# A deformable convolution pipelined with a ternary Winograd convolution: a reordered head, levelled offset taps, x1 read two chunks ahead, w1 and w2 prepared elsewhere, and no one-element memsets

## The chip, the cores and the metric

The kernel runs on one core of one Trainium2 chip. Its time is the device time of one execution in microseconds (us). The engines are TensorE (PE in the profile; PEld are its weight loads), VectorE (DVE), ScalarE (ACT), GpSimd (POOL) and SyncE (SP), which issues most DMAs; GpSimd issues the gathers.

## The reference, cut to what matters

x is (4, 256, 64, 64) in float32: 4 batches, 256 channels, 64 rows of 64 pixels. There are two layers, each on a group-normalised input and with a residual.

```python
def deform(x, w_off, b_off, w_conv):            # layer 0
    om = conv3x3(x, w_off) + b_off              # 27 channels: 18 offsets, 9 masks
    mask = sigmoid(om[:, 18:])
    # per pixel and tap k (9): a position (y, x), four neighbours, four weights
    sampled = bilinear(x, ys, xs) * mask        # zero outside the image
    return einsum("bckhw,ock->bohw", sampled, w_conv)

def ternary(w):                                 # to -1, 0, 1
    w = w - w.mean(); third = (w.max() - w.min()) / 3
    return where(w < w.min() + third, -1, where(w > w.max() - third, 1, 0))

def block(x, w1, g1, b1, w2, g2, b2):           # layer 1
    out1 = relu(batchnorm(conv3x3(x, ternary(w1)), g1, b1))
    out2 = batchnorm(conv3x3(out1, ternary(w2)), g2, b2)
    return relu(out1 + out2)

x = x + deform(group_norm(x), w_off, b_off, w_conv)
x = x + block(group_norm(x), w1, g1, b1, w2, g2, b2)
```

## The kernel before

Work is cut into chunks of 8 rows (512 pixels), 8 to a batch, 32 in all; the 256 channels are two halves of 128 partitions. The order of the work is written out by hand: each engine has a queue of its own, and semaphores tie them together. In the first part `schedule` walks over stages s = 0 to 4, and in each over 8 chunks. One chunk step does four things at once: `z`, the statistics of x for batch s+2; `o`, the offset convolution and the table of batch s+1; `d`, the sampling and the deformable convolution of batch s; `f`, the first convolution of layer 1 (Winograd, ternary weights w1) of batch s-1. Stage 4 has `f` alone. Each step is cut into nine slots k = 0 to 8, one to a tap. The loop over chunks is peeled: some chunks stand written out, the rest in a hardware loop.

*Sampling* (`d`). The normalised x stands in HBM as a table `pixel_pairs` with one row for each pixel position, which holds the four neighbours (1024 floats). For each tap GpSimd issues four indirect DMAs (L447), 128 rows of 4 KB each, into a ring `G` of 12 slots. VectorE combines them (L961): four multiply-adds 512 wide, then four 256 wide, and behind each four a one-element memset into a tile `pause` (L963). ScalarE multiplies by the last weight (L551). TensorE transposes (L1169) into `psT`, ScalarE copies that to `ST` (L607), and TensorE multiplies with `wconv` into `psD` (L1077), one tap behind the transposes. Slots of `G` come free with the transposes, three taps behind. At k = 0 `finish_deform` waits for the last tap of the chunk before, adds x (L818, into `x1c`) and takes statistics. Sampled rows go to HBM as x1.

*Offsets* (`o`). TensorE runs the nine offset taps into `psA` (L1046, `O_TAPS`: three at k=0, two at each of k=1..3). ScalarE evacuates (`om_evac`, k=4), TensorE turns (`turn_om`, k=5, L1085), ScalarE applies the sigmoid (`om_turned`, k=6), and VectorE makes row numbers and weights in two halves (`o_indices`, k=7 and k=8; L845 to L867). The convolution reads x in two parts, high and low, made by `split_hi` (ScalarE) and `split_lo` (VectorE, L771). TensorE also turns the pixels (L1196) for the table, which SyncE writes with four DMAs a chunk (`write_table`, L363).

*Head and batch 0.* Batch 0 has nobody ahead of it. In the head its statistics are taken, x is normalised in place in `G` (L496), turned (L1119) and written to the table, and its offsets are made for two chunks; for the other six, `j` work runs inside the chunk steps of stage 0, two chunks ahead: `jt_conv` at k=0..3 (`J_TAPS`, L1095), evacuation at k=4, turn at k=5, sigmoid at k=6, `jt_indices` at k=7, 8, and `jt_split` for the chunk three ahead at k=7 (L881, L888). w1 is loaded whole in the head; VectorE reduces it to sum, maximum and minimum (`weight_sums`, L668 to L670), compares (L699, L700) and transforms it there. GpSimd starts sampling when the table, its border (16 DMAs) and the indices of chunk 0 are ready. SyncE's queue in the head: x of batch 0, small constants, w1, two chunks of x of batch 1, the border, then the table rows with the other loads between them.

*Stage 4.* Eight chunks of `f`: x1 is loaded (L345) and normalised (L537), VectorE forms four planes (`planes`, L785), ScalarE copies their high part (L614), VectorE forms the low part (`planes_lo`, L794), TensorE convolves into `psF` and `psD` (L1065), and ScalarE and VectorE combine them to h1 rows (L622, L806 to L811), which SyncE stores. The load of the next chunk is issued one step ahead. In this stage w2 is loaded whole into `G`, reduced (L668 to L670, 4608 elements a partition), compared and transformed by VectorE. The second part of the kernel (L1286 on) is the second convolution and the end.

Of the kernel before, what the change touches and what calls it, by code (L numbers as in the profile page):

```python
# [14 lines left out]
def build(nc, x, w_off, b_off, w_conv, w1, w2, bn_params, ident, group_avg, sel_hl, base, out):  # L15
# [6 lines left out]
    ds = bass.ds  # L22

    NB, C, H, W = 4, 256, 64, 64
    CT = C // 128
    TAPS = 9
# [50 lines left out]
    with outer, names:  # L77
# [42 lines left out]
        with one:  # L120
# [19 lines left out]
            xres, xz = xx[:, 0], [xx[:, 3], xx[:, 1]]  # L140
# [17 lines left out]
            wst = sb(one, "wst", [128, 3, 3])  # L158
            wmm = sb(one, "wmm", [2, 4])
            wall = sb(one, "wall", [128, 8])  # L160
            pause = sb(one, "pause", [128, 2 * TAPS])
# [12 lines left out]
            ps_w_row = [psD[0:2, 0, 0:128], psT[0:2, 0, 0:128]]  # L174
            ps_w = [psD[:, 1, 0:3], psT[:, 1, 0:3]]
# [6 lines left out]
            W1_SLOT = CT * H * W // (4 * C)  # L182
            raw1 = [(0, 0, 9, g_flat[:, CT * H * W:CT * H * W + 9 * C]), (1, 0, 7, g_flat[:, CT * H * W + 9 * C:CT * H * W + 16 * C]),
                    (1, 7, 9, x1c[:, 0, :])]
            above1 = po[:, 1].rearrange("p q t h w -> p (q t h w)")[:, 0:HW]
# [12 lines left out]
            raw_off = ST[:, 0, :, :].rearrange("p t x -> p (t x)")[:, 0:CT * TAPS * 27].rearrange(  # L198
                "p (t k j) -> p t k j", t=CT, k=TAPS)
            zero_sb = xf[:, 0, :, :, :].rearrange("p t h w -> p (t h w)")[:, 0:2 * C]  # L200
# [6 lines left out]
            s_init = sem("init_steps")  # L207
            s_tern, s_wtr, s_wrd = sem("ternary_done"), sem("w_sums_step"), sem("w_sums_turned")
# [10 lines left out]
            h_stat, s_w1 = sem("h_stats_done"), sem("w1_loaded")  # L219
# [28 lines left out]
            def schedule(eng, emit):  # L248
# [3 lines left out]
                for s in range(0, NB + 1):  # L252
                    def at(r, rh, p, first, last):
# [5 lines left out]
                        just = (ahead(r, rh, p, 2), ahead(r, rh, p, 3)) if s == 0 else (None, None)  # L259
# [5 lines left out]
                        emit(s, *now, *then, *just, before)  # L265
# [43 lines left out]
            def _(sp):  # L309
                for r in range(NR):  # L310
                    sp.dma_start(x_all[:, :, r * PX:(r + 1) * PX], rows_of(x, 0, r * RC, RC)).then_inc(h_load[r], 16)
                for dst, src in ((idn[:], ident), (gavg[:], group_avg), (selhl[:], sel_hl),
                                 (base_s[:].rearrange("p r i -> p (r i)"), base.rearrange("p r i -> p (r i)")),
# [70 lines left out]
                def emit(s, z, o, d, f, o2, f2, j, j2, fp):  # L384
# [14 lines left out]
                    if f2:  # L399
                        load_f(f2)  # L400
# [1116 lines left out]
```

## Time and profile before

| | us |
|---|---|
| median of 3 runs | 2930.91 (2930.48 to 2938.26) |
| profiled execution, its own time | 2936.16 |
| span of its instructions | 2934.3 |
| head, up to the first step of VectorE in stage 0 | 117.5 |
| stage 0 | 574.0 |
| stage 1 | 531.7 |
| stage 2 | 523.2 |
| stage 3, sampling | 506.0 |
| stage 4 behind it | 167.0 |
| second part | 514.9 |
| TensorE, VectorE, ScalarE, GpSimd busy | 2442, 2234, 1275, 1368 |

An engine's busy time is the time in which it executes; TensorE's matmuls overlap, so a busy TensorE is not one at its peak. The granted clock (PEclk) is TensorE's clock as a share of 2.4 GHz. The DMA share is the mean busy share of 16 DMA engines. In a timeline a row gives the start, the time from the first start to the last end, engine, line, operation, destination and source, and the number of instructions; brackets give the idle time ahead of it and what ended it. "SPq" is SyncE issuing DMAs.

### The profile page before, as it was taken

The numbers are of one execution on the slowest core, as the hardware profiler recorded it, in microseconds if no ns is written. First come the engines' busy times: TensorE is split into PE (matmuls) and PEld (weight loads), VectorE is DVE, ScalarE is ACT, GpSimd is POOL, SyncE is SP. The second block draws the span as 40 slices with busy tenths as digits, with TensorE's granted clock in tenths as the row PEclk, the third lists the DMA queues.
The fourth block names the chain that finished last, engine by engine and source line by source line (L and its number), as shares of the span: only waits on it lengthen the run. The fifth ranks groups of instructions, "written<-read, shape, count | busy, mean of one in ns | idle before, by whom it ended". The sixth has DMA issues, their size and how long they took to land. (4 is left out here: it accounts for less than half of the span.)

```text
span 2934.3 us, 38779 instructions
## 1 busy us (share of the span) xinstructions
PE 2442.2 (83%) x12442; PEld 1692.3 (58%) x12442; DVE 2234.0 (76%) x4734; ACT 1275.2 (43%) x2181; POOL 1367.5 (47%) x1262
## 2 busy tenths in 40 slices
PE   4288888888999999999999998889887677999930
PEld 3144444444566566556566665555555677999930
DVE  6667777777888888888888887888786664666566
ACT  3244444445644445555555444444443123233245
POOL 1345554555655555556556555666652003333300
PEclk9699999999999999999999998999998888999975
DMA  7788888899999999999999999999995112111179
GB/s 248 270 292 301 317 304 303 311 348 353 332 360 354 360 351 351 342 329 363 337 361 363 343 330 325 345 347 343 342 343 218 50 61 70 53 60 52 44 278 408
DMA packets 277755, 826.29 MB, mean 282 GB/s; under 512 B 25692, under 2 KB 59484, under 8 KB 276964
## 3 DMA queue, kind: packets, MB, share of 16 engines
q0 software_dynamic: 165888, 604.05, 55.0%
q1 hardware_dynamic: 111716, 220.47, 21.7%
q8 instruction: 64, 1.05, 0.1%
q14 instruction: 87, 0.71, 0.1%
HBM read 738.95 MB, written 85.48 MB: 281 GB/s over the span
## 5 line engine op out<-in xcount | busy, mean ns | idle before, releaser
L447 POOL DMA_INDIRECT G<-pixel_pairs,quad_c x1152 | 1204.9, 1046 | 896.7 <-PE psT L1169 582.8
L961 DVE SCALAR_TENSOR_TENSOR G<-G,wts_c 128x256 f32<-128x256 f32 (+1 forms) x2304 | 1258.4, 612 | 217.5 <-DMA G<-pixel_pairs,quad_c 212.2
L1077 PE MATMUL psD<-ST,wconv 128*128 128x512 f32 x2304 | 1079.1, 613 | 0.0
L551 ACT ACTIVATE G<-G,wts_c 128x256 f32<-128x256 f32 x1152 | 490.5, 497 | 496.6 <-DVE G L961 496.5
L1077 PEld LDWEIGHTS psD<-ST,wconv 128*128 128x128 f32 x2304 | 434.6, 199 | 444.9 <-issue 444.9
L1169 PE MATMUL psT<-idn,G 128*128 128x128 f32 x2304 | 323.5, 286 | 218.8 <-ACT G L551 216.6
L607 ACT ACTIVATE ST<-psT 128x1024 f32<-128x1024 f32 x288 | 294.1, 1021 | 419.4 <-PE psT L1169 419.2
L1169 PEld LDWEIGHTS psT<-idn,G 128*128 128x128 f32 x2304 | 269.8, 146 | 314.7 <-ACT G L551 185.2
L1065 PE MATMUL psF<-pl,qw 128*128 128x256 f32 x1872 | 267.6, 298 | 35.7 <-DVE h1c L809 24.9
L1065 PEld LDWEIGHTS psF<-pl,qw 128*128 128x128 f32 x1872 | 244.2, 195 | 53.3 <-DVE h1c L809 21.2
L1046 PE MATMUL psA<-po,woff 128*64 128x512 f32 x864 | 253.2, 437 | 0.0
L1474 PE MATMUL psG<-po,qw 128*128 128x256 f32 x1440 | 226.8, 286 | 24.7 <-POOL po L1325 24.7
L1474 PEld LDWEIGHTS psG<-po,qw 128*128 128x128 f32 x1440 | 197.8, 191 | 24.9 <-issue 24.9
L1046 PEld LDWEIGHTS psA<-po,woff 128*64 128x64 f32 x864 | 117.0, 136 | 108.0 <-issue 39.6
L1348 ACT ACTIVATE po<-area 128x1024 fp32r<-128x1024 f32 x48 | 49.2, 1056 | 250.8 <-PE psG L1474 242.2
L1474 PE MATMUL psG<-pg,qw 128*128 128x256 f32 x864 | 141.8, 285 | 0.0
L1325 POOL TENSOR_TENSOR po<-area,po 128x1024 fp32r<-128x1024 f32 x32 | 69.9, 2206 | 123.0 <-ACT po L1348 123.0
L818 DVE TENSOR_TENSOR x1c<-psD,xx 128x1024 f32<-128x1024 f32 x32 | 39.2, 1224 | 114.2 <-PE psD L1077 114.2
L1474 PEld LDWEIGHTS psG<-pg,qw 128*128 128x128 f32 x864 | 124.4, 189 | 0.0
L1402 DVE TENSOR_TENSOR area<-area 128x512 f32<-128x512 f32 x128 | 79.9, 686 | 51.2 <-POOL pg L1325 25.5
L561 ACT ACTIVATE yT<-psX 128x256 f32<-128x256 f32 x96 | 36.2, 377 | 167.3 <-PE psX L1196 166.8
L785 DVE TENSOR_TENSOR xx<-xf 128x512 f32<-128x512 f32 x128 | 80.0, 685 | 30.1 <-ACT xf L537 29.6
(214 smaller groups left out, 2241.0 us busy)
## 6 DMA issues: line engine op xcount, KB each, us to landing
xx<-in_x SPq DMA_DIRECT2D x56, 512.0 KB, 4.3
pixel_pairs<-yT SPq DMA_DIRECT2D x104, 256.0 KB, 7.2
G<-pixel_pairs,quad_c POOLq DMA_INDIRECT x1152, 6.6
x<-x1c SPq DMA_DIRECT2D x32, 512.0 KB
h<-h1c SPq DMA_DIRECT2D x32, 512.0 KB, 9.1
out<-h SPq DMA_DIRECT2D x16, 1024.0 KB, 17.3
xf<-x SPq DMA_DIRECT2D x24, 640.0 KB, 8.5
area<-h SPq DMA_DIRECT2D x24, 640.0 KB, 4.1
```

The lines of the kernel that those rows point to most:

```text
L447: pool.indirect_dma_start(out=G[:, i % RING, :], out_offset=None, in_=tbl[d.b].rearrange("y x q c -> (y x) (q c)"), in_offset=bass.Indirec ...
L551: act.activation(g, g, ACT.Copy, scale=wts_c[:, d.p, i:i + 1]).then_inc(d_scaled, 1)
L607: act.activation(ST[:, k % 3], psT[:], ACT.Copy).then_inc(d_st, 1)
L785: i = dve.tensor_tensor(V[:, :, j], xf[:, f.p, :, a:a + 7:2, :], xf[:, f.p, :, b:b + 7:2, :], op)
L961: dve.scalar_tensor_tensor(g[:, 0:w], g[:, w:2 * w], wts_c[:, d.p, q * NG + i:q * NG + i + 1], g[:, 0:w], ALU.mult, ALU.add).then_inc(d_ma ...
L1046: ins = pe.matmul(acc[:, oc, :].rearrange("p (h w) -> p h w", h=RC), w[:, t, tap, oc * m:(oc + 1) * m], pad[:, c.p, part, t, dy:dy + RC, d ...
L1065: ins = pe.matmul(acc[:, bank, half * 256:half * 256 + 256].rearrange("p (h w) -> p h w", w=W), w[:, oc * 128:(oc + 1) * 128], p[:, part, ...
L1077: ins = pe.matmul(psD[:, oc, :], wconv[:, t, k, oc * 128:(oc + 1) * 128], ST[:, k % 3, t, :], start=(k == 0 and t == 0), stop=(k == TAPS - ...
L1169: ins = pe.transpose(psT[:, c, t * 128:(t + 1) * 128], G[:, (PT * k + t) % RING, c * 128:(c + 1) * 128], idn[:])
L1325: i = pool.tensor_tensor(pg(c.p, 1, t)[:, :, 1:W + 1], V[:, t].rearrange("p j i w -> p (j i) w"), pg(c.p, 0, t)[:, :, 1:W + 1].bitcast(F32 ...
L1402: i = dve.tensor_tensor(V[:, :, j], xg[:, c.p, :, a:a + 2 * RP - 1:2, :], xg[:, c.p, :, b:b + 2 * RP - 1:2, :], op)
L1474: i = pe.matmul(psG[:, c.p, oc, j, :].rearrange("p (h w) -> p h w", h=RP), w[:, oc * 128:(oc + 1) * 128], pg(c.p, part, t)[:, RP * j:RP * ...
```

## The change

In the sampling the memsets into `pause` are gone. In the head, VectorE takes statistics before any constant is needed, and the offset weights are split behind them. SyncE loads small constants first, then x; it loads four chunks of batch 1 at once into four buffers, then x for offset chunk 2, then writes the border of batch 0 alone; the borders of the other batches and `wconv` come behind the table. w1 is no longer in the head: it is loaded in six pieces (twice, once for the reductions and once for the comparison), and VectorE works on two pieces at a time in stage 0: reductions at k=3 of chunks 0, 3 and 4, comparisons at k=1 and k=6 of chunk 6 and k=6 of chunk 7, the transform at k=7 of chunk 7. Offset taps are spread anew, the offset work of batch 0 is shifted by half a step, and both halves of `o_indices` stand at k=8. w2 is reduced in six pieces in stage 3 (chunks 4 and 5, k=1, 3, 5); its comparison and transform run on GpSimd at the start of stage 4. In stage 4 x1 is loaded and normalised two chunks ahead. Stages 3 and 4 are peeled by five chunks instead of three.

VectorE's memset, and the walk and the taps:

```diff
-                                dve.memset(pause[:, 2 * k + q - 1:2 * k + q], 0.0)
...
-                    walk(eng, at, 5 if s == 0 else 3)
-            J_TAPS = {0: [0, 1], 1: [2, 3], 2: [4, 5], 3: [6, 7, 8]}
-            O_TAPS = {0: [0, 1, 2], 1: [3, 4], 2: [5, 6], 3: [7, 8]}
+                    walk(eng, at, 3 if 0 < s < NB - 1 else 5)
+            J_TAPS = {5: [0, 1], 6: [2, 3], 7: [4, 5], 8: [6, 7, 8]}
+            O_TAPS = {0: [0], 1: [1, 2], 2: [3, 4], 3: [5, 6], 4: [7, 8]}
```

SyncE, head:

```diff
+                for dst, src in ((idn[:], ident), (gavg[:], group_avg)):
+                    sp.dma_start(dst, src).then_inc(s_small, 16)
                 for r in range(NR):
                     sp.dma_start(x_all[:, :, r * PX:(r + 1) * PX], rows_of(x, 0, r * RC, RC)).then_inc(h_load[r], 16)
...
-                    for t, k0, k1, raw in raw1:
-                        sp.dma_start(raw, w1.rearrange("(t c) k o -> c t (k o)", c=128)[:, t, k0 * C:k1 * C]).then_inc(s_w1, 16)
-                    load_z(Chunk(1, 0, 0, 0, True, False))
-                    load_z(Chunk(1, 1, 0, 1, False, False))
-                    table_border()
+                    for r in range(4):
+                        load_hz(r)
+                    load_j(Chunk(0, 2, 1, 0, False, False))
+                    sp.wait_ge(s_zero, 6)
+                    table_border(0, s_edge)
                     for r in range(NR):
                         sp.wait_ge(h_yt, 2 * (r + 1))
                         write_table(0, r, yt_ring[r % 4], h_tw[r % 4])
...
+                        if r < 4:
+                            load_hz(r + 4)
+                        if r == 4:
+                            load_o(Chunk(1, 0, 0, 0, True, False))
+                    sp.dma_start(wconv[:].rearrange("p t k o -> p (t k o)"),
+                                 w_conv.rearrange("(t c) k o -> c t (k o)", c=128)).then_inc(s_wconv, 16)
+                    for b in range(1, NB):
+                        table_border(b, s_edge_rest)
+                    sp.wait_ge(z_stat, 2 * NR + CREDIT)
+                    load_w1(0)
```

SyncE, each step:

```diff
-                    if f2:
+                    if f2 and (s < NB or f.first):
                         load_f(f2)
+                    if s == NB and f2 and not f2.last:
+                        load_f(f2.after())
```

GpSimd:

```diff
+                def w2_ternary():
+                    pool.wait_ge(s_lim, 1)
+                    pool.wait_ge(s_wraw, 16)
+                    pool.tensor_scalar(above2, stage2, wall[:, 3:4], wall[:, 6:7], ALU.subtract, ALU.is_gt)
+                    pool.tensor_scalar(stage2, stage2, wall[:, 3:4], wall[:, 5:6], ALU.subtract, ALU.is_lt).then_inc(s_w2, 1)
+                    pool.wait_ge(s_w2, 1)
+                    pool.tensor_tensor(above2, above2, stage2, ALU.subtract).then_inc(s_w2, 1)
...
+                    pool.tensor_tensor(both, g[0], g[2], ALU.add).then_inc(s_w2, 1)
+                    pool.wait_ge(s_w2, 3)
+                    pool.tensor_tensor(minus, both, g[1], ALU.subtract)
+                    pool.tensor_tensor(g[1], both, g[1], ALU.add).then_inc(s_w2, 1)
+                    pool.wait_ge(s_w2, 4)
+                    pool.tensor_scalar(minus, minus, 0.5, None, ALU.mult)
+                    pool.tensor_scalar(g[1], g[1], 0.5, None, ALU.mult).then_inc(s_tern, 1)
```

ScalarE, each step:

```diff
+                        if jp and k == 1:
+                            jt_om_evac(jp)
+                        if j and k == 1:
+                            jt_normalise(j)
+                        if jp and k == 3:
+                            jt_om_turned(jp)
-                        if o and k == 4:
+                        if o and k == 5:
                             om_evac(o)
...
-                        if o and k == 6:
+                        if o and k == 7:
                             om_turned(o)
```

VectorE, each step:

```diff
+                        if s == NB - 1 and k in (1, 3, 5) and (d.is_row(4) or d.is_row(5)):
+                            part = k // 2 + (3 if d.is_row(5) else 0)
+                            dve.wait_ge(s_w2l, 48 if d.is_row(4) else 96)
+                            weight_sums(part, w2_part[k // 2]).then_inc(s_w2p, 1)
...
-                        if o and k in (7, 8):
-                            o_indices(o, k - 7)
-                        if j and k in (7, 8):
-                            jt_indices(j, k - 7)
-                        if j2 and k == 7:
-                            jt_split(j2, xf_rows(j2))
+                        if o and k == 8:
+                            o_indices(o, 0)
+                            o_indices(o, 1)
+                        if j and k == 2:
+                            jt_split(j, xf_rows(j))
+                        if jp and k in (4, 5):
+                            jt_indices(jp, k - 4)
+                        if s == 0 and k == 3:
+                            for r, p0, loaded in ((0, 0, 32), (3, 2, 64), (4, 4, 96)):
+                                if d.is_row(r):
+                                    dve.wait_ge(s_w1, loaded)
+                                    for part in (p0, p0 + 1):
+                                        weight_sums(part, w1_part[part % 2]).then_inc(s_w1p, 1)
...
+                        if s == 0:
+                            for r, kk, p0, loaded in ((6, 1, 0, 128), (6, 6, 2, 160), (7, 6, 4, 192)):
+                                if d.is_row(r) and k == kk:
+                                    dve.wait_ge(s_w1, loaded)
+                                    compare_w1(p0)
+                                    compare_w1(p0 + 1)
+                        if s == 0 and k == 7 and d.is_row(7):
+                            dve.wait_ge(s_w1p, 12)
+                            winograd_w1()
```

TensorE, each step:

```diff
-                            if k == 5 and j:
-                                jt_turn_om(j)
-                            if k == 5:
+                            if k == 2 and jp:
+                                jt_turn_om(jp)
+                            if k == 6:
                                 pe.wait_ge(o_yt, PT * (o.n + 1))
```

## Rows read from the trace of the kernel before

**Rows 1.** Busy time of each engine by stretch, granted clock, DMA share, GB/s

```profile
core 0: us, PE busy (x) PEld busy (x) DVE busy (x) ACT busy (x) POOL busy (x), PEclk, DMA share, GB/s
0.00:117.50 117.50, 35.94 (x161) 25.49 (x161) 77.05 (x147) 30.68 (x49) 15.72 (x16) 0.80 0.71 232
117.50:566.20 448.70, 372.62 (x1427) 209.38 (x1428) 327.93 (x812) 189.00 (x365) 229.35 (x227) 0.92 0.85 308
...
691.50:1223.20 531.70, 495.64 (x2301) 313.75 (x2300) 458.39 (x1056) 272.67 (x501) 305.31 (x299) 0.99 0.94 351
...
2252.40:2419.40 167.00, 111.98 (x800) 110.34 (x798) 110.79 (x153) 40.38 (x52) 0.05 (x1) 0.83 0.22 73
```

**Rows 2.** Timeline of the head

```profile
17.62 1.02 DVE L660 MEMSET woff<- 128x1152 f32 x1 [17.62 <-DMA boff<-in_b_off]
...
19.77 9.59 DVE L902 BATCH_NORM_STATS2 st<-G 128x6 f32<-128x512 f32 x16
...
32.58 4.34 ACT L496 ACTIVATE G<-G,bij,scj 128x512 f32<-128x512 f32 x6 [0.43 <-DVE bij L760]
...
102.24 4.29 SPq L363 DMA_DIRECT2D pixel_pairs<-yT  x4
...
110.31 0.21 POOL L440 COPY quad_c<-quad 128x36 int32<-128x36 int32 x1 [99.10 <-DMA pixel_pairs<-yT]
```

**Rows 3.** Timeline of TensorE in chunk 3 of batch 0

```profile
352.49 3.09 PE L1046 MATMUL psA<-po,woff 128*64 128x512 f32 x12
...
396.79 3.60 PE L1077 MATMUL psD<-ST,wconv 128*128 128x512 f32 x8
402.73 1.09 PE L1169 MATMUL psT<-idn,G 128*128 128x128 f32 x8 [2.35 <-ACT G L551]
403.66 5.29 PE L1077 MATMUL psD<-ST,wconv 128*128 128x512 f32 x8
416.15 1.97 PE L1169 MATMUL psT<-idn,G 128*128 128x128 f32 x8 [7.19 <-ACT G L551]
```

**Rows 4.** Timeline of VectorE in the same chunk, tap 8

```profile
411.22 3.14 DVE L961 SCALAR_TENSOR_TENSOR G<-G,wts_c 128x512 f32<-128x512 f32 x5
```

**Rows 5.** Timeline of TensorE in chunk 4 of batch 1

```profile
976.10 1.09 PE L1169 MATMUL psT<-idn,G 128*128 128x128 f32 x8 [0.77 <-ACT G L551]
...
1023.15 1.09 PE L1169 MATMUL psT<-idn,G 128*128 128x128 f32 x8 [1.75 <-ACT G L551]
...
1033.85 0.38 PE L1169 MATMUL psT<-idn,G 128*128 128x128 f32 x2
```

**Rows 6.** Timeline of stage 4

```profile
2283.09 4.93 DVE L668 TENSOR_REDUCE wst<-G 128x1 f32<-128x4608 f32 x1
...
2306.69 5.47 PE L1065 MATMUL psF<-pl,qw 128*128 128x256 f32 x24 [14.13 <-DVE h1c L809]
...
2398.97 5.40 PE L1065 MATMUL psF<-po,qw 128*128 128x256 f32 x24 [4.93 <-DVE h1c L809]
```

**Rows 7.** Timeline of VectorE, batch 1, five multiply-adds in a row

```profile
1027.30 3.15 DVE L961 SCALAR_TENSOR_TENSOR G<-G,wts_c 128x512 f32<-128x512 f32 x5
```

**Rows 8.** DMA issues: KB each, median us from issue to landing

```profile
G<-in_x SPq DMA_DIRECT2D x8, 512.0 KB, 7.7
```

**Rows 9.** Busy time by stretch, behind TensorE's wait in chunk 3

```profile
404.00:407.00 3.00, 3.00 (x5) 1.21 (x4) 2.67 (x10) 0.89 (x1) 2.30 (x3) 0.50 1.02 407
```

**Rows 10.** VectorE's groups in stage 4: busy, mean ns, idle

```profile
L699 DVE TENSOR_SCALAR G<-G,wall 128x4608 f32<-128x4608 f32 x1 | 2.7, 2678 | 0.0
```

**Rows 11.** GpSimd's groups

```profile
L1325 POOL TENSOR_TENSOR po<-area,po 128x1024 fp32r<-128x1024 f32 x32 | 69.9, 2206 | 123.0 <-ACT po L1348 123.0
...
L423 POOL MEMSET po<- 128x5280 f32 x1 | 4.5, 4512 | 0.0
```

**Rows 12.** Timeline of GpSimd, two gathers

```profile
120.55 0.94 POOL L447 DMA_INDIRECT G<-pixel_pairs,quad_c  x1 [0.30 <-issue]
121.80 1.40 POOL L447 DMA_INDIRECT G<-pixel_pairs,quad_c  x1 [0.31 <-issue]
```

More of the change, by code:

```diff
@@ L258, in at @@
                             then = (now[1] and now[1].after(), now[3] and now[3].after())
-                        just = (ahead(r, rh, p, 2), ahead(r, rh, p, 3)) if s == 0 else (None, None)
+                        just = [ahead(r, rh, p, n) if s == 0 else None for n in (2, 3, 1)]
                         f, before = now[3], None
@@ L404, in emit @@
                         load_j(j2)
+                    if s == 0 and d.is_row(6):
+                        sp.wait_ge(s_w1p, 8)
+                        load_w1(2)
                     if o:
@@ L442, in emit @@
                     for i in range(NG):
-                        if s == 0 and d.first and i == W1_SLOT:
-                            hold(pool, s_tern, 1)
                         if i % PT == RING % PT:
@@ L592, in emit @@
                     if f and not d:
+                        if f2 and not f2.last:
+                            normalise(f2.after(), xf, f_load, sc1, bi1, f_y, None)
                         h1_begin(s, f, 1)
@@ L672, in weight_sums_ready @@
                 def weight_sums_ready(parts):
-                    for part in range(1, parts):
-                        dve.tensor_tensor(wst[:, 0, 0:1], wst[:, 0, 0:1], wst[:, 0, part:part + 1], ALU.add)
-                        dve.tensor_tensor(wst[:, 1, 0:1], wst[:, 1, 0:1], wst[:, 1, part:part + 1], ALU.max)
-                        step(dve.tensor_tensor(wst[:, 2, 0:1], wst[:, 2, 0:1], wst[:, 2, part:part + 1], ALU.min))
-                    dve.tensor_scalar(wst[:, 2, 0:1], wst[:, 2, 0:1], -1.0, None, ALU.mult).then_inc(s_wtr, 1)
+                    for m, op in enumerate((ALU.add, ALU.max, ALU.min)):
+                        ins = dve.tensor_reduce(wst[:, m, 6:7], wst[:, m, 0:parts], AX.X, op)
+                    step(ins)
+                    dve.tensor_scalar(wst[:, 2, 6:7], wst[:, 2, 6:7], -1.0, None, ALU.mult).then_inc(s_wtr, 1)
                 def weight_extremes(m):
@@ L722, in compare_w1 @@
-                def compare_w1(part):
-                    t, k0, k1, raw = raw1[part]
-                    above = above1[:, 0:(k1 - k0) * C]
-                    compare(above, raw)
-                    step(dve.tensor_tensor(qw[:, t, k0:k1, :].rearrange("p k o -> p (k o)"), above.bitcast(F32), raw, ALU.subtract))
+                    dve.tensor_tensor(q, q.bitcast(F32), raw, ALU.subtract).then_inc(s_w1p, 1)
+                def winograd_w1():
+                    for t in range(CT):
+                        q = [qw[:, t, 3 * y:3 * y + 3, :].rearrange("p k o -> p (k o)") for y in range(3)]
+                        both, mid = w1_part
+                        dve.tensor_tensor(both, q[0].bitcast(F32), q[2].bitcast(F32), ALU.add)
+                        step(dve.tensor_scalar(mid, q[1].bitcast(F32), 0.5, None, ALU.mult))
+                        dve.scalar_tensor_tensor(wino[:, t].rearrange("p k o -> p (k o)"), both, 0.5, mid, ALU.mult, ALU.subtract)
+                        step(dve.scalar_tensor_tensor(q[1], both, 0.5, mid, ALU.mult, ALU.add))
+                    dve.sem_inc(s_tern, 1)
```

269 lines of the change are left out of this document (134 added, 135 removed).

## The prediction, made before the changed kernel was run

> **What bounds the kernel now.** I read the busy times by stretch first [rows 1], to see which engine has room in which stage. In the sampling of batch 1 TensorE is busy 495.6 of 531.7 us, and the DMA engines 0.94 of the time at 351 GB/s: two limits close together. In the first six chunks of batch 0 TensorE has 372.6 of 448.7 us and the DMA engines 0.85, so an order inside the chunk is at fault. In the stretch without sampling, 167 us, TensorE is busy 112 and the DMA engines 0.22. In the head TensorE works 35.9 of 117.5 us and VectorE 77.1.
>
> Then the timelines. In the head VectorE does nothing until 17.62 us, when the last small constant lands; its statistics begin at 19.77, ScalarE's first normalised rows at 32.58, and GpSimd's first copy of row numbers waits until 110.31 for the table, whose last row took SyncE 4.29 us for four DMAs [rows 2]. In a chunk of batch 0 TensorE waits 2.35 us for tap 7 and 7.19 for tap 8 [rows 3]: VectorE has splits and two halves of index chains between taps 7 and 8, and starts tap 8 at 411.22 only [rows 4]. In a chunk of batch 1 the waits are 0.77 us at tap 1 and 1.75 at tap 8 [rows 5]. In the last stretch chunk 2 begins at 2306.69, after a wait of 14.13 us, behind weight reductions that began at 2283.09, and chunk 7 at 2398.97: 18.5 us for each of five chunks [rows 6].
>
> **The change part by part.**
>
> *Memsets.* 576 go. One is queued between the fourth 512-wide and the first 256-wide multiply-add, and those five run in 3.15 us without a gap [rows 7]. The 0.06 us lie in the shadow of the neighbours; I take 0. Bounds: 0, and 576 x 0.06 = 34 us of gain were each on the path.
>
> *Head.* Statistics no longer wait for constants. The x loads land 7.7 us after issue in the median [rows 8], the last at about 15; with one pair of statistics behind it the chain is some 12.5 us earlier, and the first rows are normalised at 20. The x load for offset chunk 2 now stands in SyncE's queue ahead of all table writes and waits for the first offset split: 20, 3 for the second row, 3 for the split, is 26. Four border writes make it 30.5. Eight rows at 4.29 and five loads of 0.6 between them give 68, the last lands 4.5 later: 72.5, 37 us earlier than before. For loads that share the DMA engines with the first rows I take back 1: **-36** (-44 to -26). VectorE's weight work leaves the head too, but is paid below.
>
> *Batch 0, order inside the chunk.* The next batch's offset taps go from 3,2,2,2 to 1,2,2,2,2, this batch's from k=0..3 to k=5..8; splits and index chains are spread. The waits at taps 7 and 8 go (9.5 us) and the slowed deform taps behind them: after the wait of 2.35 the granted clock is 0.50, the level of 1.2 GHz, for a while [rows 9], and eight matmuls take 5.29 us, not 3.60 [rows 3]; two such spells, 3.4. What is late next is tap 1. It needs x1, statistics and its multiply-adds from VectorE, 7.6 us after tap 0, whatever TensorE has; taking two offset taps of either kind from k=0 (three take 3.09 us, so four 4.1) is a wait there of 5.6 us, and one slowed tap, 1.7. A chunk has 448.7/6 = 74.8 us, some 73.8 without the first one's start-up: 73.8 - 9.5 - 3.4 + 4.1 + 1.7 = 66.7. DMA: 308 GB/s x 74.8 us is 23.0 MB a chunk; with 0.6 MB of w1 (twelve pieces of 0.39 in eight chunks) at batch 1's 351 GB/s it is 67.3. I take 67.5; six chunks, -6.3 each: -38.
>
> *w1 inside batch 0.* A reduction of 4608 elements takes 4.93 us [rows 6], of 768 then 0.82; three for each of two pieces are 5 us, behind tap 3 of chunks 0, 3 and 4. TensorE has 6.7 us for that tap, VectorE's tap is 4.3: 1 to 3 us of each show, +5. A comparison is two tensor_scalars at 2.68 per 4608 [rows 10] and a tensor_tensor at the reduction's rate; two pieces 3.9 us with their steps, twice in chunk 6: +5. In chunk 7 a pair, the transform (6.7), the whole index chain and a split stand behind taps 6 to 8: +10. Batch 0 together: **-18** (-45 to 0).
>
> *Batches 1 and 2.* At k=0 two offset taps (2.1 us) go, but tap 1 waits for VectorE already [rows 5], so the wait grows to 2.8; that of 2.35 us had a lowered clock behind it, so I put +1.0 as a mean over chunks. k=4 gets 2.1 more. The first index half leaves k=7, so the 1.75 at tap 8 goes. Late next could be tap 0 of the next chunk: whole chain (4.8), h1 rows (2.5) and the tap (5.2) are 12.5 us behind tap 8; TensorE needs 10.7 from there to 1033.85, and VectorE's lead should cover the rest. Net +1.1 x 16: **+18** (-5 to +35).
>
> *Batch 3.* w2 in six pieces, 2.5 us each, behind taps 1, 3 and 5 of two chunks. TensorE waits for VectorE there, so about 5 us a chunk show: **+9** (+3 to +15).
>
> *Last stretch.* x1 loaded and normalised two ahead takes the load out of the loop of planes, copy, remainder and rows. TensorE alone needs 112/800 us x 96 matmuls = 13.4 a chunk [rows 1], at the mixed clock; at the full one 13.1. Five chunks from 18.5 to 13.3 are -26, the wait of 14.13 shrinks to 1.3, -13: -39. New: w2's ternary on GpSimd, 12288 elements of tensor_scalar and 9216 of tensor_tensor. GpSimd's two-input operation takes 2.206 us per 1024, its memset 4.51 per 5280 [rows 11]: tensor_tensor 20 us, tensor_scalar between 10 and 26, in all 38 +- 8. Does VectorE go on under it? One gather took 0.94 us, the next, issued under a two-input VectorE operation, 1.40 [rows 12]: it waited for the other to end. If that holds in the other direction too, each long GpSimd operation lets one of the six two-input operations of chunk 2's planes through; they would be done some 30 us late, and TensorE has nothing else by then. Bounds -39 and 0; I take the exclusion, the nearest row: **-10** (-42 to 0). Part two is untouched.
>
> The Trainium skill (SBUF — State Buffer, section Who interferes with whom) says that a VectorE instruction with two SBUF inputs and a GpSimd instruction that reads SBUF exclude each other for the whole instruction, whichever is first. Rows 12 agree in one direction; by the rule the last stretch is worth -10, without it -39.
>
> Sum: -36 -18 +18 +9 -10 = -37. The profiled execution has 2936.2 us, 1.9 more than its span, so 2899; the runs' median is 5.2 lower, so 2894. I say **2892**.
>
> **The rivals.**
> 1. VectorE runs on beside GpSimd in the last stretch. For it: no two-input VectorE row is seen waiting for GpSimd. -66 in all: 2865.
> 2. Batches 0 to 2 come out better: the clock stays high and VectorE's lead absorbs w1: batch 0 -32, batches 1 and 2 +4. With the exclusion: 2866. Against it: 2.35 us was enough to lower the clock once.
> 3. Batch 0 keeps its length: w1's work meets a chain with no lead, and the DMA engines, already at 0.94 in batch 1, are the limit. Batch 0 at 0: 2912. Against it: the wait of 7.19 us is VectorE's, and that work is spread.
> 4. Slower: VectorE's tail at k=8. If the offsets' turn (evacuated at k=5, turned at k=6, sigmoid at k=7) comes late, or VectorE has no lead, the index chain, h1 rows and tap 0 hold TensorE in 24 chunks. The gain of 37 is cancelled at 1.5 us a chunk and it is slower by 0.3% from 1.9; at 2.5 us it is 2892 + 60 = 2952. For it: 12.5 us of VectorE against 10.7 of TensorE. Against: VectorE ends tap 8 earlier by what left k=7.
> 5. The memsets mattered: without them gathers find no room between multiply-adds. 1.2 us a chunk x 32 cancels the gain: 2931. Against: a gather under multiply-adds got in at the next boundary [rows 12].
>
> **How the numbers follow.** Forecast 0.40, rival 1 0.22, rival 2 0.12, rival 3 0.14, rival 4 0.08, rival 5 0.04. The range runs from 2846 (rivals 1 and 2 in part together) to 2922 (rival 3 with batches 1 and 2 at +28). 0.3% is 8.8 us, about what a measurement of this kernel can tell from no change. Slower: rival 4, 0.08; within: rival 5 and the edge of rival 3, 0.06; faster 0.86.
>
> **What the profile after would show.** GpSimd's first copy of row numbers at 70 to 76 us. Chunks of batch 0 of 66 to 69 us, 5 us of wait at tap 1 and a lowered clock behind it, none at tap 8. In batch 1 about 3 us at tap 1. In the last stretch VectorE's plane subtractions waiting beside GpSimd's 5 to 10 us operations, the chunks behind them 13 to 14 us apart. The prediction is wrong if table writes start before 26 or after 35, if tap 0 waits in batches 1 and 2, or if a GpSimd tensor_scalar costs more than a tensor_tensor.

## The result and the profile after

The changed kernel is slower: 2962.9 us, median of 6 runs (2952.4 to 2965.7), beside 2934.6 for the kernel before on the same chip (2930.2 to 2940.4). The ratio is 1.0091, 95% interval 1.0075 to 1.0107. The forecast was 2892, range 2846 to 2922.

Where the time went is read from VectorE's first step in each batch, in the profiled execution of each kernel (us; the last three columns stop at the last deform matmul, at the first load of the second part, and at the end):

| | head | batch 0 | batch 1 | batch 2 | batch 3 | last stretch | second part |
|---|---|---|---|---|---|---|---|
| before | 117.5 | 574.0 | 531.6 | 523.2 | 506.1 | 170.2 | 511.7 |
| after | 70.1 | 567.0 | 562.5 | 546.6 | 536.8 | 167.4 | 512.3 |
| difference | -47.4 | -7.0 | +30.9 | +23.4 | +30.7 | -2.8 | +0.6 |
| forecast | -36 | -18 | +18 for both | | +9 | -10 | 0 |

The head and batch 0 together are 54 shorter, as forecast. The three batches behind them are 85 longer where 27 were forecast. So I read first the busy times of the changed kernel by stretch (head; chunks 1 to 5 of batch 0; batch 1; last stretch), which answer to [rows 1]:

```profile
0.00:70.10 70.10, 33.62 (x148) 23.57 (x148) 36.51 (x85) 27.92 (x44) 10.66 (x10) 0.88 0.85 267
153.10:489.00 335.90, 308.99 (x1208) 174.92 (x1207) 285.26 (x619) 159.48 (x306) 211.49 (x186) 0.96 0.93 345
637.10:1199.60 562.50, 506.87 (x2296) 319.44 (x2295) 459.08 (x912) 271.99 (x501) 358.74 (x297) 0.97 0.90 329
2283.00:2450.40 167.40, 103.13 (x797) 102.23 (x797) 128.19 (x146) 40.72 (x53) 63.88 (x12) 0.81 0.21 73
```

In batch 1 VectorE has as much work as before (459 us), and the DMA engines are less busy (0.90, not 0.94). GpSimd, the fifth engine in the row (POOL), went from 305 to 359 us, with the same 288 gathers to issue. Its groups say what grew; first the kernel before, then after (columns: line, engine, operation, count, busy us, mean ns, then idle time ahead and what ended it):

```profile
L447 POOL DMA_INDIRECT G<-pixel_pairs,quad_c x1152 | 1204.9, 1046 | 896.7 <-PE psT L1169 582.8 <-issue 300.3 <-POOL quad_c L440 13.7
```

```profile
L502 POOL DMA_INDIRECT G<-pixel_pairs,quad_c x1152 | 1412.5, 1226 | 762.8 <-PE psT L1221 438.6 <-issue 303.3 <-POOL quad_c L497 20.0
```

A gather takes 1.226 us in the mean instead of 1.046, 208 us more over 1152, and the time in which GpSimd waits for free slots (`<-PE psT`) is what shrank. The mean hides the shape. Sorted by duration, the longest gather before has 1.98 us; after, 59 have over 2.5 us, up to 8.58, and these 59 hold 250 us. One of them, GpSimd's timeline and then VectorE's:

```profile
1426.16 1.15 POOL L502 DMA_INDIRECT G<-pixel_pairs,quad_c  x1 [0.31 <-issue]
1427.61 7.13 POOL L502 DMA_INDIRECT G<-pixel_pairs,quad_c  x1 [0.30 <-issue]
1435.04 0.94 POOL L502 DMA_INDIRECT G<-pixel_pairs,quad_c  x1 [0.30 <-issue]
```

```profile
1426.41 5.11 DVE L994 SCALAR_TENSOR_TENSOR G<-G,wts_c 128x256 f32<-128x256 f32 x10
1431.44 2.49 DVE L827 TENSOR_TENSOR xx<-xf 128x512 f32<-128x512 f32 x4
1433.85 0.41 DVE L848 TENSOR_TENSOR h1c<-h1c,psF 128x256 f32<-128x256 f32 x1
```

A gather takes 0.94 us if nothing is in its way [rows 12]. This one ends at 1434.74; 0.94 back from there is 1433.80, within 0.13 us of where the four plane subtractions end. For 6 us seven multiply-adds and four subtractions, all with two operands in SBUF, follow each other without a gap, and GpSimd gets in at none of the boundaries between them. Of the 59 long gathers 5 lie in batch 0, which has no plane subtractions beside the multiply-adds, and 19, 14 and 21 in batches 1 to 3. VectorE pays later: its wait for gathered rows ahead of the multiply-adds, 212.2 us in the kernel before, is 241.2 us:

```profile
L994 DVE SCALAR_TENSOR_TENSOR G<-G,wts_c 128x256 f32<-128x256 f32 (+1 forms) x2304 | 1257.2, 612 | 244.7 <-DMA G<-pixel_pairs,quad_c 241.2 <-DVE wts_c L980 1.2 <-DVE qw L767 0.2
```

The head, to hold beside [rows 2]: the statistics begin at 6.05, the first rows are normalised at 20.20, the table writes begin at 28.78 and GpSimd's first copy of row numbers stands at 73.31. The last row is VectorE's first multiply-add, which waits 12.66 us for a gather; in the kernel before that wait is 1.71 us.

```profile
6.05 1.29 DVE L944 BATCH_NORM_STATS2 st<-G 128x6 f32<-128x512 f32 x2 [3.04 <-DMA G<-in_x]
...
20.20 4.34 ACT L549 ACTIVATE G<-G,bij,scj 128x512 f32<-128x512 f32 x6 [0.43 <-DVE bij L802]
...
28.78 4.11 SPq L376 DMA_DIRECT2D pixel_pairs<-ST  x4
...
73.31 0.21 POOL L497 COPY quad_c<-quad 128x36 int32<-128x36 int32 x1 [62.10 <-DMA pixel_pairs<-yT]
...
82.97 0.75 DVE L994 SCALAR_TENSOR_TENSOR G<-G,wts_c 128x512 f32<-128x512 f32 x1 [12.66 <-DMA G<-pixel_pairs,quad_c]
```

In the chunks TensorE's wait stands at tap 1, in batch 0 (first row) and smaller in batch 1 (second); in batch 1 the deform matmuls behind it take 4.25 us instead of 3.60, at a granted clock of 0.61 from 939.4 to 941.0. These answer to [rows 3] and [rows 5]. The last row is VectorE in batch 0's last chunk, at the comparison of w1:

```profile
237.60 1.97 PE L1221 MATMUL psT<-idn,G 128*128 128x128 f32 x8 [5.38 <-ACT G L601]
...
937.58 1.97 PE L1221 MATMUL psT<-idn,G 128*128 128x128 f32 x8 [2.68 <-ACT G L601]
939.34 4.25 PE L1132 MATMUL psD<-ST,wconv 128*128 128x512 f32 x8
...
611.31 0.73 DVE L754 TENSOR_SCALAR qw<-xx,wall 128x768 fp32r<-128x768 f32 x1 [7.13 <-DMA xx<-in_w]
```

Last, the last stretch, GpSimd, VectorE, TensorE; it answers to [rows 6]:

```profile
2315.73 15.89 POOL L466 TENSOR_SCALAR G<-G,wall 128x4608 f32<-128x4608 f32 x1 [51.91 <-DVEq L1072]
2331.63 16.70 POOL L467 TENSOR_SCALAR G<-G,wall 128x4608 f32<-128x4608 f32 x1
2348.42 10.74 POOL L469 TENSOR_TENSOR G<-G 128x4608 f32<-128x4608 f32 x1
...
2299.06 2.50 DVE L827 TENSOR_TENSOR xx<-xf 128x512 f32<-128x512 f32 x4 [1.28 <-ACT xf L587]
...
2315.89 16.78 DVE L827 TENSOR_TENSOR xx<-xf 128x512 f32<-128x512 f32 x4 [0.33 <-DVE wall L749]
2334.74 14.50 DVE L836 TENSOR_TENSOR pl<-xx,pl 128x1024 fp32r<-128x1024 f32 x2 [2.07 <-ACT pl L667]
...
2350.77 4.46 PE L1120 MATMUL psF<-pl,qw 128*128 128x256 f32 x24 [27.23 <-DVE h1c L851]
...
2381.10 4.64 PE L1120 MATMUL psF<-po,qw 128*128 128x256 f32 x24 [17.08 <-DVE h1c L851]
...
2394.34 3.09 PE L1120 MATMUL psF<-pl,qw 128*128 128x256 f32 x24
...
2406.07 3.08 PE L1120 MATMUL psF<-po,qw 128*128 128x256 f32 x24
```

Four subtractions take 2.50 us alone and 16.78 us beside GpSimd's comparison, which begins 0.16 us ahead of them; TensorE then waits 27.23 and 17.08 us. Once GpSimd is done, at 2379.4, one more chunk takes 13.2 us and those behind it 11.7 each.

### The profile page after: what moved, and what is told of

Read it like the earlier page. It is cut to its first block and busy times, and to the rows that moved or that the text cites. A ratio compares the mean times of both kernels' runs of the same rounds, so it can differ in the third digit from the quotient of the medians.

```text
span 2962.7 us, 37580 instructions
## 1 busy us (share of the span) xinstructions
PE 2466.9 (83%) x12442; PEld 1703.2 (57%) x12442; DVE 2261.2 (76%) x4186; ACT 1276.0 (43%) x2181; POOL 1639.0 (55%) x1270
## 5 line engine op out<-in xcount | busy, mean ns | idle before, releaser
L502 POOL DMA_INDIRECT G<-pixel_pairs,quad_c x1152 | 1412.5, 1226 | 762.8 <-PE psT L1221 438.6
L994 DVE SCALAR_TENSOR_TENSOR G<-G,wts_c 128x256 f32<-128x256 f32 (+1 forms) x2304 | 1257.2, 612 | 244.7 <-DMA G<-pixel_pairs,quad_c 241.2
L1132 PE MATMUL psD<-ST,wconv 128*128 128x512 f32 x2304 | 1095.6, 620 | 0.0
L1132 PEld LDWEIGHTS psD<-ST,wconv 128*128 128x128 f32 x2304 | 442.3, 202 | 452.4 <-issue 451.5
L1221 PE MATMUL psT<-idn,G 128*128 128x128 f32 x2304 | 334.5, 292 | 248.5 <-ACT G L601 245.4
L1221 PEld LDWEIGHTS psT<-idn,G 128*128 128x128 f32 x2304 | 279.2, 150 | 333.6 <-ACT G L601 226.6
L1101 PE MATMUL psA<-po,woff 128*64 128x512 f32 x864 | 267.7, 450 | 0.0
L827 DVE TENSOR_TENSOR xx<-xf 128x512 f32<-128x512 f32 x128 | 109.5, 916 | 1.9 <-ACT xf L587 1.3
L1383 POOL TENSOR_TENSOR pg<-area,po 128x1024 fp32r<-128x1024 f32 x16 | 35.5, 2218 | 115.5 <-ACT pg L1406 115.5
```

Source lines behind the costliest of these rows:

```text
L502: pool.indirect_dma_start(out=G[:, i % RING, :], out_offset=None, in_=tbl[d.b].rearrange("y x q c -> (y x) (q c)"), in_offset=bass.Indirec ...
L827: i = dve.tensor_tensor(V[:, :, j], xf[:, f.p, :, a:a + 7:2, :], xf[:, f.p, :, b:b + 7:2, :], op)
L994: dve.scalar_tensor_tensor(g[:, 0:w], g[:, w:2 * w], wts_c[:, d.p, q * NG + i:q * NG + i + 1], g[:, 0:w], ALU.mult, ALU.add).then_inc(d_ma ...
L1101: ins = pe.matmul(acc[:, oc, :].rearrange("p (h w) -> p h w", h=RC), w[:, t, tap, oc * m:(oc + 1) * m], pad[:, c.p, part, t, dy:dy + RC, d ...
L1132: ins = pe.matmul(psD[:, oc, :], wconv[:, t, k, oc * 128:(oc + 1) * 128], ST[:, k % 3, t, :], start=(k == 0 and t == 0), stop=(k == TAPS - ...
L1221: ins = pe.transpose(psT[:, c, t * 128:(t + 1) * 128], G[:, (PT * k + t) % RING, c * 128:(c + 1) * 128], idn[:])
```

## The experiments

Four theories were open (the expectations, written before each run, use further letters and say there what they stand for). A: the memsets were the breaks at which gathers got in. B, its rival: the order inside the chunks is what costs. D and F: the w2 work in batch 3, and the w2 work on GpSimd in the last stretch. Times are medians; the ratio is to the kernel before, with its 95% interval.

**1 and 2. The memsets put back, and taken out of the kernel before.**

```diff
+            om_cf = sb(one, "om_c", [128, PX])
+            om_c, pause = om_cf[0:64, :], om_cf[64:128, 0:4 * TAPS]
...
+                                dve.memset(pause[:, 2 * k + q - 1:2 * k + q], 0.0)
```

> The changed kernel with the one-element memset back behind each four multiply-adds. Theory A (the memsets were the breaks at which a gather's instruction got in: in the changed kernel 59 gathers take over 2.5 us, up to 8.6, and the mean is 1.226 us, while before none took over 2.0 and the mean was 1.046): mean back to 1.03 to 1.08, none over 2.5 us, VectorE's waits for gathers in batches 1 and 2 down from 7 to 10 us a chunk to 5, and the time falls from 2963 to 2890 to 2915. Theory B (the offset taps and the two index halves at k=8 make batches 1 to 3 longer, whatever the memsets): the gathers may get shorter, the time stays at 2955 to 2963.

2947.6 us, 1.0062 (1.0045 to 1.0079). The gathers are as before (mean 1.039, one over 2.5 us), but only 15 us came back between the medians, and by the ratios, which allow for the two chips, 9: a miss of the 2890 to 2915 that theory A gave. The reason is in this run's own memsets: for want of room they went to partitions 64 to 127 of another tile, and there each moved the next multiply-add back by 0.21 us (start to start 0.877 us, not 0.663). So the run shows that the memsets let gathers in, and hides what that is worth.

```diff
-                                dve.memset(pause[:, 2 * k + q - 1:2 * k + q], 0.0)
```

> The kernel before with the memsets alone left out. Theory A: gathers wait through trains of multiply-adds here too, mean over 1.15 us, batches 1 to 3 longer by 15 to 25 us each, 2970 to 3000. Theory B: nothing changes, 2925 to 2935.

3018.7 us, 1.0305 (1.0288 to 1.0322): 88 us lost by leaving out instructions that a profile books at 34 us, and more than the 2970 to 3000 expected. The gathers' mean is 1.195 us; 48 have over 2.5 us. No offset tap, load or weight was moved here, so theory A holds by itself. The profiled execution, the fastest of the four, is 75 us longer than the kernel before's; the loss lies in batches 1 to 3 (566.3, 543.9 and 527.3 us), and head and batch 0 keep their lengths within 1.1 us.

**3 and 4. Another break, and more breaks** (both still on partitions 64 to 127).

```diff
+                                dve.tensor_tensor(pause[:, 2 * k + q - 1:2 * k + q], wts_c[64:128, d.p, 0:1], wts_c[64:128, d.p, 1:2], ALU.add)
```

> The changed kernel with a one-element add of two SBUF operands in the place of each memset. Theory A in its form 'two-input instructions of VectorE keep the gather out, and only another kind between them lets it in': the train is not broken, gathers over 2.5 us remain about 59, mean about 1.2, time 2955 to 2975. Rival A2 (any boundary that is longer or any short instruction is a break): as with the memsets, 2890 to 2915.

2967.0 us, 1.0127 (1.011 to 1.0143); one gather over 2.5 us, mean 1.057. So a two-input instruction can be a break. The gain in time that this should have brought is hidden again: each add moved the next multiply-add back by 0.29 us. And like run 1's memset this add begins only when the multiply-add ahead of it has ended, so the fair test of the kind of instruction is run 9.

```diff
+                                    if t % 2:
+                                        dve.memset(pause[:, 4 * k + 2 * q + t // 2 - 2:4 * k + 2 * q + t // 2 - 1], 0.0)
```

> The changed kernel with a memset behind every two multiply-adds, four to a tap. Theory A: the longest wait of a gather under multiply-adds falls below 1.5 us, mean gather 0.98 to 1.03; those behind plane subtractions stay. 576 more memsets cost at most 0.014 us each, 8 us. Time within 6 us of the run with two memsets to a tap. Theory B: 2955 to 2970.

3011.8 us, 1.0286 (1.0269 to 1.0303), against the expectation: the expectation priced a memset at 0.014 us and it was 0.21. 576 more of them cost 64 us in time, half of their 121 us on VectorE. The gathers missed as well: none over 2.5 us, but a mean of 1.084, not 0.98 to 1.03. More breaks did not make the mean shorter.

**5. The memsets as before had them,** on all 128 partitions of a tile of their own.

```diff
+            pause = sb(one, "pause", [128, 2 * TAPS])
...
+                                dve.memset(pause[:, 2 * k + q - 1:2 * k + q], 0.0)
```

> The changed kernel with the memsets back over all 128 partitions, as before had them. In the run with memsets over partitions 64 to 127 each of them moved the next multiply-add back by 0.21 us (0.877 from start to start against 0.663), where before's moved it by 0.00 to 0.01. Theory A: here they cost as little as before, VectorE's tap is 4.3 us again, no gather is over 2.5 us, and the time is 2905 to 2930: below the run with half the partitions by 20 us or more. Theory B (order of slots is all): 2940 to 2950, no gain over that run.

2909.3 us, 0.9910 (0.9883 to 0.9938). With these two lines the changed kernel is 53.6 us faster than without it, and faster than the kernel before. The gathers' row, and VectorE's wait for them, 157.3 us instead of 241.2:

```profile
L503 POOL DMA_INDIRECT G<-pixel_pairs,quad_c x1152 | 1210.4, 1051 | 905.1 <-PE psT L1223 601.0 <-issue 290.5 <-POOL quad_c L498 12.7
...
L995 DVE SCALAR_TENSOR_TENSOR G<-G,wts_c 128x256 f32<-128x256 f32 (+1 forms) x2304 | 1255.6, 612 | 160.6 <-DMA G<-pixel_pairs,quad_c 157.3 <-DVE wts_c L981 1.2 <-DVE qw L768 0.2
```

**12. The same tile, partitions 64 to 127 alone.**

```diff
+                                dve.memset(pause[64:128, 2 * k + q - 1:2 * k + q], 0.0)
```

> The changed kernel with the memsets into the same tile as in the run with 128 partitions, but over partitions 64 to 127 alone. Theory G (the partitions are what made each memset of the first run cost 0.21 us of VectorE): start to start of the 512-wide and the first 256-wide multiply-add across a memset is 0.87 us, 2940 to 2950. Rival (the place in the other tile did it): 0.66 to 0.67 us, 2905 to 2915.

2951.2 us, 1.0060 (1.0040 to 1.0079): it is the partitions, not the place in another tile. A memset on all partitions lies under the multiply-adds (the first three rows, run 5: five of them run in 3.15 us, as in [rows 7], and the memset stands inside that time). On partitions 64 to 127 it begins only when the fourth multiply-add has ended (run 12) and the fifth comes behind it. That is 0.21 us each, 121 us of VectorE over 576, of which 42 show in the time:

```profile
1000.72 3.15 DVE L995 SCALAR_TENSOR_TENSOR G<-G,wts_c 128x512 f32<-128x512 f32 x5
1003.41 0.06 DVE L997 MEMSET pause<- 128x1 f32 x1
1003.79 1.94 DVE L995 SCALAR_TENSOR_TENSOR G<-G,wts_c 128x256 f32<-128x256 f32 x4
```

```profile
1001.05 2.73 DVE L995 SCALAR_TENSOR_TENSOR G<-G,wts_c 128x512 f32<-128x512 f32 x4
1003.84 0.06 DVE L997 MEMSET pause<- 64x1 f32 x1
1003.91 1.67 DVE L995 SCALAR_TENSOR_TENSOR G<-G,wts_c 128x256 f32<-128x256 f32 x4
```

No run separates the number of partitions (64, not 128) from where they start (64, not 0). A row of the changed kernel speaks for the start: of two steps on the 2-partition tile `wmm`, the second ends at 2205.13, and the multiply-add behind it begins at 2205.05 all the same:

```profile
2204.60 0.28 DVE L736 TENSOR_REDUCE wmm<-psA 2x1 f32<-2x128 f32 x1
2204.92 0.22 DVE L737 TENSOR_SCALAR wmm<-idn,wmm 2x2 f32<-2x2 f32 x1
2205.05 0.73 DVE L994 SCALAR_TENSOR_TENSOR G<-G,wts_c 128x512 f32<-128x512 f32 x1
```

Nor is it the delay that lets gathers in: in run 5 a memset delays VectorE by 0.01 us, and one gather in 1152 is over 2.5 us, as in runs 1 and 12 with 0.21.

**8 and 9. Fewer breaks, and a two-input break at its cheap price** (the tile `pause` as in run 5).

```diff
+                                if q == 2:
+                                    dve.memset(pause[:, k:k + 1], 0.0)
```

> The changed kernel with one memset a tap, behind the fourth 256-wide multiply-add; none between the 512-wide and the 256-wide ones. The longest unbroken stretch of two-input work is then eight multiply-adds, or plane and h1 work with them, where the long waits (4 to 8.6 us in the changed kernel) ended behind 4 to 14 instructions. Theory A1 (what counts is a break between the multiply-adds and the work behind them): nearly all long gathers go, 2905 to 2920. A2 (both breaks are needed): gathers of 2.5 to 4 us stay, 2925 to 2945.

2909.9 us, 0.9915 (0.9898 to 0.9931): the same as with two. Half the memsets are enough; one gather has over 2.5 us, 23 have 1.6 to 2.5.

```diff
+                                dve.tensor_tensor(pause[:, 2 * k + q - 1:2 * k + q], wts_c[:, d.p, 0:1], wts_c[:, d.p, 1:2], ALU.add)
```

> The changed kernel with a one-element add of two SBUF operands over all 128 partitions in the place of each memset. In the run with 64 partitions it broke the trains (one gather over 2.5 us), but cost 0.28 us of VectorE each. Theory E (any short instruction is a break, its price is its own time): no long gathers, each add moves the next multiply-add back by 0.07 to 0.16 us, 41 to 92 us of VectorE in all of which a third shows: 2920 to 2945. Rival (cheap as the memset): 2905 to 2915.

2926.8 us, 0.9971 (0.9961 to 0.9980). Each add costs 0.07 us, and 13 gathers have over 2.5 us (mean 1.118), where none was expected: a break, but a worse one. How the 17.5 us above run 5 divide between its 40 us of VectorE and the 77 us of longer gathers, these runs don't tell.

**6. The old offset slots.**

```diff
-            O_TAPS = {0: [0], 1: [1, 2], 2: [3, 4], 3: [5, 6], 4: [7, 8]}
+            O_TAPS = {0: [0, 1, 2], 1: [3, 4], 2: [5, 6], 3: [7, 8]}
...
-                        if o and k == 8:
-                            o_indices(o, 0)
-                            o_indices(o, 1)
+                        if o and k in (7, 8):
+                            o_indices(o, k - 7)
```

(with evacuation, turn and sigmoid one slot earlier, and the memsets as in run 5)

> As the run with memsets over 128 partitions, with the offset work of the next batch in its old slots too (taps 3,2,2,2 from k=0, evacuation at 4, turn at 5, sigmoid at 6, index halves at 7 and 8). Theory C (these slots are what lengthens batches 1 and 2 beyond the memsets): batch 1 back to 532 to 536 us, batch 2 to 523 to 527, batch 0 longer by 0 to 10; in all 10 to 25 us below the run with the new slots. Rival: the slots change nothing by more than 5 us, and what is left comes from the other moved work.

2891.7 us, 0.9853 (0.9828 to 0.9878), 17.6 below run 5. Batch 1 has 532.1 us, not 543.6, batch 2 525.1, not 530.4; batch 0 keeps 563.1 (563.5 in run 5), so its gain over the kernel before does not come from these slots. Theory B (C in this expectation) is true as well, with a third of the size of A.

**7. w2's reductions on one column** (on top of run 5). Each reads one element a partition and leaves out the other 767.

```diff
-                            weight_sums(part, w2_part[k // 2]).then_inc(s_w2p, 1)
+                            weight_sums(part, w2_part[k // 2][:, 0:1]).then_inc(s_w2p, 1)
```

> As the run with memsets over 128 partitions, but the reductions of w2 in batch 3 read one column and not 768 (so w2's ternary values are wrong); loads and waits stay. Theory D (the 18 reductions show nearly whole): chunks 4 and 5 of batch 3 fall from 66 to 73 us to 61 to 63, the time by 12 to 18 us. Rival (they lie in VectorE's waits, as half of them do in the forecast): by 0 to 9 us.

2897.1 us, 0.9873 (0.9848 to 0.9898), 12.2 below run 5; batch 3 has 509.7 us instead of 520.0. Chunk 5 falls from 65.2 to 58.4, chunk 4 only from 68.2 to 66.1 (61 to 63 expected for both). In run 5 the 18 reductions follow each other at 0.87 us, 15.7 in all; most of that shows.

**10. w2's comparison and transform on VectorE,** in pieces behind chunks 0, 3, 4, 5 and 6 of the last stretch (on top of run 6).

```diff
-                    if s == NB and f.first:
-                        w2_ternary()
...
+                        dve.tensor_scalar(above2, stage2, wall[:, 3:4], wall[:, 6:7], ALU.subtract, ALU.is_gt)
+                    if s == NB and f.is_row(3):
+                        step(dve.tensor_scalar(stage2, stage2, wall[:, 3:4], wall[:, 5:6], ALU.subtract, ALU.is_lt))
...
+                    if s == NB and f.is_row(4):
+                        step(dve.tensor_tensor(above2, above2, stage2, ALU.subtract))
```

> As the run with the memsets and the old offset slots, with w2's comparison and transform on VectorE in the last stretch (16.5 us in pieces behind chunks 0, 3, 4, 5 and 6) and not on GpSimd. Theory F (VectorE's plane subtractions wait for GpSimd: four took 16.8 us instead of 2.5, and TensorE waited 27 and 17 us): these waits go, the stretch falls from 168 to 125 to 140 us, the time from 2892 to 2850 to 2865. Rival (the 16.5 us on VectorE take the place of the waits): 160 to 168, 2885 to 2892.

2852.1 us, 0.9712 (0.9696 to 0.9728): the fastest of all. The last stretch falls from 167.8 to 133.7 us. The same comparison that took GpSimd 15.89 us takes VectorE 2.68, the four subtractions behind it 2.49, and TensorE waits 3.11:

```profile
2243.89 2.68 DVE L1072 TENSOR_SCALAR G<-G,wall 128x4608 f32<-128x4608 f32 x1
2246.48 2.49 DVE L826 TENSOR_TENSOR xx<-xf 128x512 f32<-128x512 f32 x4
...
2254.94 4.63 PE L1132 MATMUL psF<-pl,qw 128*128 128x256 f32 x24 [3.11 <-DVE h1c L850]
```

**11. w2's reductions at slots 5, 6 and 7** (on top of run 10).

```diff
-                        if s == NB - 1 and k in (1, 3, 5) and (d.is_row(4) or d.is_row(5)):
+                        if s == NB - 1 and k in (5, 6, 7) and (d.is_row(4) or d.is_row(5)):
```

> As the run before it, with w2's reductions in batch 3 behind taps 5, 6 and 7 of chunks 4 and 5, not behind 1, 3 and 5: VectorE's lead over TensorE's transposes is 2.5 to 4.3 us at taps 6 to 8 and 0.6 at taps 1, 3 and 5. Expected: of the 12 us that the reductions cost 4 to 8 go, 2845 to 2860. Rival (a later piece then holds tap 8 or the next tap 0): no gain within 3 us.

2859.6 us, 0.9748 (0.9732 to 0.9765), 7.5 slower than run 10 between the medians: the gain of 4 to 8 us did not come. In the profiled executions, which have the same span (2856.6), chunks 4 and 5 take 73.4 and 66.8 us instead of 69.6 and 65.7. VectorE now waits for ScalarE's h1 rows there (first row). The other two are SyncE's stores of h1 rows, in run 11 and in run 10, each right behind the second load of w2:

```profile
2009.63 0.42 DVE L847 TENSOR_TENSOR h1c<-h1c,psF 128x256 f32<-128x256 f32 x1 [8.00 <-ACT h1c L674]
...
1998.89 0.45 SPq L440 DMA_DIRECT2D h<-h1c  x1
...
1988.91 0.40 SPq L440 DMA_DIRECT2D h<-h1c  x1
```

SyncE holds the second load of w2 until the first three pieces are summed, and the store of h1 rows that frees `h1c` is queued behind that load. Summed later, it is stored later: issued at 1998.89, landed at 2009.14, and VectorE goes on at 2009.63. That explains the wait, not the 7.5 us: batch 3 as a whole has 520.5 us here and 520.7 in run 10, so the difference between the medians lies in executions that no trace shows.

## Why the prediction was wrong, step by step

**The step that failed is "Memsets": "The 0.06 us lie in the shadow of the neighbours; I take 0."** The price of the instructions was right (0.01 us each, run 5), the worth of what they did for another engine was not. It was rival 5, at 0.04, and dismissed by one pair of rows: a gather under multiply-adds got in at the next boundary [rows 12]. Most do. But with the memsets gone one in 20 takes 2.5 to 8.6 us and gets in at none of the boundaries that pass. The bounds given for the term were 0 and a gain of 34 us. The loss stood only in rival 5, at 38 us, so the sum could not see it. Measured: 53.6 us in the changed kernel (run 5 against it), 88 in the kernel before (run 2). Here 59 gathers have over 2.5 us, there 48, so it isn't their count that sets the price; what does is open. By batch the worth in the changed kernel is 3.5, 18.9, 16.2 and 16.8 us (its lengths less run 5's).

**The offset slots in batches 1 and 2**, forecast +18: run 5 against before gives +12.0 and +7.2, so +19, and run 6 takes 16.8 of these back. The mechanism was as written: tap 1 waits 2.2 us instead of 0.6 in batch 1 (mean of seven chunks in run 5), the wait of 1.6 at tap 8 is gone.

**Head and batch 0**, forecast -36 and -18: -47.4 and -7.0. The table writes began at 28.8 (30.5 forecast), the first copy at 73.3 (70 to 76 forecast). Against run 5 the sum is -57.5. That copy is 37.0 earlier than before, so the head's term was right; the cut between it and batch 0 was drawn badly. VectorE leaves the head before the first rows are gathered and waits 12.66 us, not 1.71, so the first chunk takes 83.0 us, not 73. Chunks 1 to 5 are 33.4 us shorter (31.7 forecast, less 5 for w1), with 5.4 us of wait at tap 1. The last two are 22.7 longer, not 15: in chunk 7 VectorE stood 7.13 us for the load of the last two pieces of w1, a wait for which the forecast had no term.

**w2 in batch 3**, forecast +9: +13.9 in run 5. A reduction of 768 elements takes 0.87 us from start to start, not 0.82 as scaled from 4608, and of the 15.7 us of 18 of them 10.3 (batch 3's length) to 12.2 (the medians) show in run 7, where 10 were forecast. The other 3.6 us of the 13.9 are open.

**The last stretch**, forecast -10 as -39 +30: the exclusion is what happened: VectorE waits for GpSimd here, where in the batches GpSimd waits for VectorE. That both are one mechanism fits the rows; no run shows it. GpSimd's eight operations took 63 us, not 38: the tensor_tensors 22 (20 forecast), but the tensor_scalars 41, outside the bounds of 10 and 26 and by the forecast's own words a sign that it is wrong; the two of 4608 elements alone took 15.9 and 16.7. A subtraction of 0.68 us that began 0.16 us behind the first of them took 14.97. The three behind it then took 0.68 each, so it isn't one VectorE operation to each of GpSimd's, as forecast. Run 10 prices it at 34 us of the stretch and 39.6 between the medians. The chunks behind came 11.7 us apart and not 13.3, which gave some of it back; in the end -2.8. The forecast's 13.1 at the full clock was wrongly worked out: 13.4 at the mean clock of 0.83 in [rows 1] scales to 11.1. The Trainium skill (SBUF — State Buffer, section Who interferes with whom) has a VectorE instruction with two SBUF inputs and a GpSimd instruction that reads SBUF exclude each other, the second fully blocked until the first finishes. The 14.97 us agree. The 7.13 us of the gather above go further, as it waited through eleven instructions and not one. The same section infers that `tensor_tensor` with both inputs in SBUF does not hold up descriptor generation. The gathers here were held up under such instructions and under multiply-adds; but a gather also reads its row numbers (`quad_c`) from SBUF, and no run tells which part of its work had to wait.

Put together: with the memsets kept, the other terms give -25 in run 5's span (2909.0) where -37 was forecast, inside the range. One term, taken as nothing, was worth more than the sum of all others.

**What stays open.** Which boundary lets a gather in. Of the 76 gathers over 1.9 us in the changed kernel, 20 were let in when VectorE stood idle, 18 ahead of an h1 row addition that reads PSUM, 26 between a plane or split subtraction and a multiply-add, 9 between a multiply-add and an instruction of another kind (statistics, a memset, the index chain), and 3 between two instructions of one kind. That gathers can wait long in trains of two-input instructions, and that memsets between them end this, is shown; why most gathers enter such a train at once is not.

## What to carry to other kernels

An instruction that does nothing may be there for another engine: before it is deleted as free, look at the spread of durations of what shares SBUF with it, not the mean, and put a loss among its bounds. Where VectorE runs long trains of instructions with two SBUF operands while GpSimd gathers, one one-element memset over all 128 partitions between them is worth trying. And elementwise work that is moved from a busy VectorE to GpSimd may not be out of VectorE's way: on GpSimd it made this kernel 39.6 us longer than the same work on VectorE, where it takes 16.5 us.

## What the runs showed of the hardware that was not expected

- A gather's instruction of 0.94 us waited up to 7.6 us more behind up to 14 back-to-back VectorE instructions with two SBUF operands (changed kernel). With a one-element memset behind each four or each eight multiply-adds one in 1152 had over 2.5 us (runs 5 and 8).
- A one-element memset on 128 partitions moved the next multiply-add by 0.00 to 0.01 us (before, run 5), on partitions 64 to 127 by 0.21 us (0.877 against 0.663 from start to start, runs 1 and 12); a one-element add of two SBUF operands on 128 partitions by 0.07 us (run 9), on partitions 64 to 127 by 0.29 us (run 3).
- GpSimd's tensor_scalar on 128 x 4608 took 15.9 and 16.7 us, its tensor_tensor of the same size 10.7 us (changed kernel, with VectorE at work beside it); VectorE's took 2.68 and 4.94 us (run 10).
